# Node tiles of 124 rows instead of 128 in a four-layer graph kernel, without products of one row, and with the adjacency's row sums moved

## The reference

```python
# layer 0: two GRU cells, one on adj0 @ h, one on three attention heads (adj0 = adj without its diagonal)
edge_support = sum over heads of softmax(where(adj0 > 0, e_plus, -inf)) * adj0 @ hW, divided by 3
# layer 1: degree-normalised product
adj_norm = rowsum**-0.5 * adj * rowsum**-0.5 ; out = (adj_norm @ x) @ W.T + b
# layer 2: two attention heads over (adj + I) > 0, softmax over a row, elu
# layer 3: four attention heads over adj > 0.5, softmax over a column, bias
```

## Time and profile before

| | |
|---|---|
| median of 3 runs | 2648.63 us (2644.78 to 2657.8) |
| profiled execution, its own time | 2668.64 us |
| its span, first to last instruction | 2666.8 us |
| busy: PE / DVE / ACT / POOL | 2231.1 / 1563.6 / 768.5 / 252.2 us |
| mean granted TensorE clock | 0.882 of full speed |
| moved by DMA | 271.72 MB, mean 102 GB/s |

### The profile page before, as it was taken

One profiled execution on the slowest core, in us unless ns is written; L12 is line 12 of the kernel. 1 busy time (PEld: TensorE's weight loads), 2 busy tenths in 40 slices (PEclk: granted clock), 3 DMA queues, 4 the chain that ended last, 5 costly groups with the idle time before them and its releaser, 6 DMA issues. The chain is left out here.

```text
span 2666.8 us, 25438 instructions
## 1 busy us (share of the span) xinstructions
PE 2231.1 (84%) x9760; PEld 1184.0 (44%) x9760; DVE 1563.6 (59%) x2517; ACT 768.5 (29%) x1013; POOL 252.2 (9%) x128
## 2 busy tenths in 40 slices
PE   4889997068989999996999679977999845999991
PEld 2445555023434343445655334446999431222231
DVE  3323331566666766642577743345777256989787
ACT  0122221487777787743222100001000010000000
POOL 0000000000000000000000000000000005656440
PEclk9989995579999999998999889988989567989895
DMA  3366552334444444336000044421000004323211
GB/s 121 146 200 208 198 188 89 127 139 149 158 145 157 153 157 160 115 115 205 1 0 1 0 111 132 131 68 43 9 17 9 30 22 156 95 73 94 58 53 42
DMA packets 131908, 271.72 MB, mean 102 GB/s; under 512 B 14044, under 2 KB 44506, under 8 KB 127922
## 3 DMA queue, kind: packets, MB, share of 16 engines
q1 hardware_dynamic: 113458, 240.71, 28.4%
q10 hardware_dynamic: 18324, 29.34, 2.9%
HBM read 226.64 MB, written 43.37 MB: 101 GB/s over the span
## 5 line engine op out<-in xcount | busy, mean ns | idle before, releaser
L706 PE MATMUL banks<-arena 128*128 128x512 f32 (+3 forms) x1584 | 650.7, 570 | 57.8 <-DVE arena L1262 55.5
L706 PEld LDWEIGHTS banks<-arena 128*128 128x128 f32 (+1 forms) x1584 | 294.1, 199 | 412.7 <-issue 401.8
L1480 DVE SCALAR_TENSOR_TENSOR arena<-arena 128x1024 f32<-128x1024 f32 (+3 forms) x264 | 323.6, 1300 | 38.8 <-PE banks L842 20.2
L1262 DVE TENSOR_TENSOR arena<-arena 128x1536 f32<-128x1536 f32 (+2 forms) x132 | 206.8, 1567 | 170.6 <-ACT arena L964 170.5
L803 PE MATMUL banks<-arena 128*128 128x129 f32 (+2 forms) x1936 | 266.5, 300 | 5.1 <-DVE arena L1437 5.1
L803 PEld LDWEIGHTS banks<-arena 128*128 128x128 f32 (+2 forms) x1936 | 237.7, 202 | 36.8 <-issue 26.8
L765 PE MATMUL banks<-arena 128*128 128x512 f32 (+2 forms) x528 | 209.5, 548 | 45.6 <-DVE arena L1355 44.1
L667 PE MATMUL banks<-arena 128*128 128x512 f32 (+2 forms) x528 | 244.3, 591 | 0.0
L830 PE MATMUL banks<-arena 128*64 128x512 f32 (+3 forms) x1056 | 228.1, 570 | 12.8 <-DVE arena L1480 12.8
L572 POOL TENSOR_SCALAR arena<-arena 128x1024 bf16<-128x1024 f32 (+1 forms) x66 | 210.4, 3189 | 144.6 <-DVE arena L1480 136.8
L1437 DVE SCALAR_TENSOR_TENSOR arena<-arena 128x512 f32<-128x512 f32 (+2 forms) x264 | 169.9, 686 | 89.6 <-PE banks L803 77.0
(11 more groups left out here) (177 smaller groups left out, 1959.4 us busy)
## 6 DMA issues: line engine op xcount, KB each, us to landing
arena<-adj_T SPq DMA_DIRECT2D x210, 256.0 KB, 3.1
arena<-hw_rows SPq DMA_DIRECT2D x126, 384.0 KB
arena<-in_adj SPq DMA_DIRECT2D x21, 1354.0 KB
adj_T<-arena ACTq DMA_DIRECT2D x105, 256.0 KB, 2.6
arena<-in_adj SPq DMA_DIRECT2D x25, 1024.0 KB
arena<-in_adj SPq DMA_DIRECT2D x42, 512.0 KB
hw_rows<-arena SPq DMA_DIRECT2D x1, 8064.0 KB
arena<-in_adj SPq DMA_DIRECT2D x21, 330.0 KB
```

What stands on the lines that cost most here:

```text
L706: ins = PE.matmul(bank(2 * (c % 2) + f)[:, 0:wid(c)], hs[0:kp(t), n % 3, h * D + f * P:h * D + (f + 1) * P], E[0:kp(t), n % 3, h, 0:wid(c) ...
L1262: V.tensor_tensor(e, e, strips[n % 4][0:k, 0:w].unsqueeze(1).to_broadcast([k, H0, w]), ALU.mult).then_inc(s["p_ok"], 1)
L1480: V.scalar_tensor_tensor(PM3[0:k, n % 2, h, 0:w], r3_bc[0:k, h, c * WW:c * WW + w], smalls[0:k, 4, h * T + t:h * T + t + 1], mask3[0:k, n ...
```

## The change

A new constant R = 124 takes the place of P wherever P meant the rows of a node tile. T stays 22, but the last tile has 104 rows instead of 20; a chunk has W = 496 columns instead of 512, and the last one 228 instead of 148. The numbers of units, of products and of transfers stay as they are. Stage 3 keeps its chunks of 1024 columns. `opened` now multiplies 128 rows of zeros and closes itself (`start=True, stop=True`), `closed` is gone, and stage 2 has no opening product at all: the first product into a bank carries `start`. `row_sum` on ACT is gone; instead VectorE reduces each block of stage A to four partial sums, and the reader of the next block waits for it (`summed`).

```diff
+R = 124
-T = -(-N // P)
-TAIL = N - (T - 1) * P
+T = -(-N // R)
+TAIL = N - (T - 1) * R
 RPC = 4
-W = RPC * P
+W = RPC * R
...
-WW = 2 * W
+BANK = 512
+WW = 2 * BANK
...
 def kp(t):
-    return P if t < T - 1 else TAIL
+    return R if t < T - 1 else TAIL
...
         def load_nodes(eng, dst, src, s):
-            load(eng, dst[:, 0:T - 1, :], src[0:(T - 1) * P, :].rearrange("(t p) d -> p t d", p=P), s)
-            load(eng, dst[0:TAIL, T - 1, :], src[(T - 1) * P:N, :], s)
+            load(eng, dst[0:R, 0:T - 1, :], src[0:(T - 1) * R, :].rearrange("(t p) d -> p t d", p=R), s)
+            load(eng, dst[0:TAIL, T - 1, :], src[(T - 1) * R:N, :], s)
...
             if i >= 2:
                 sp.wait_ge(sw["A"]["transposed"], WideLoad(i - 2).units_after)
+                sp.wait_ge(sw["A"]["summed"], i - 1)
...
-            load(sp, arow[0:kp(i), :], adj[i * P:i * P + kp(i), :], b_in)
+            load(sp, arow[0:kp(i), :], adj[i * R:i * R + kp(i), :], b_in)
...
         def opened(b):
-            PE.matmul(bank(b), zrow[0:1, 0:P], zrow[0:1, :], start=True, stop=False)
-
-        def closed(b):
-
-            return PE.matmul(bank(b), zrow[0:1, 0:P], zrow[0:1, :], start=False, stop=True)
+            PE.matmul(bank(b), zrow[:, 0:P], zrow, start=True, stop=True)
...
                         ins = PE.matmul(bank(b0 + k // 3)[0:nr, (k % 3) * (C2 + 1):(k % 3 + 1) * (C2 + 1)],
-                                        PM2[0:kp(t), n % 3, h, r * P:r * P + nr], proj2[0:kp(t), t, h, :],
-                                        start=False, stop=False, skip_group_check=True)
-                if t == T - 1:
-                    for b in range(3):
-                        ins = closed(b0 + b)
+                                        PM2[0:kp(t), n % 3, h, r * R:r * R + nr], proj2[0:kp(t), t, h, :],
+                                        start=k // 3 not in begun, stop=t == T - 1, skip_group_check=True)
+                        begun.add(k // 3)
...
-            def row_sum(i):
-                act.wait_ge(b_diag, i + 1)
-                S.activation(arow[0:kp(i), :], arow[0:kp(i), :], ACT.Copy, accum_out=rowsum[0:kp(i), i:i + 1]
-                             ).then_inc(b_sum, 1)
...
+            def row_sums(ld):
+                dve.wait_ge(s["wide_in"][ld.buf], ld.landed)
+                if ld.k == ld.c:
+                    dve.wait_ge(s["diag_ok"], ld.c * RPC + tiles_in(ld.c))
+                if ld.c < CH - 1:
+                    ins = V.tensor_reduce(rpart[0:R, ld.c * RPC:(ld.c + 1) * RPC, ld.k], ablk[0:R, ld.buf, :, 0:ld.width], AX_X, ALU.add)
+                else:
+                    for r, nr in enumerate(rows_in(ld.c)):
+                        ins = V.tensor_reduce(rpart[0:nr, ld.c * RPC + r, ld.k:ld.k + 1], ablk[0:nr, ld.buf, r, 0:ld.width], AX_X, ALU.add)
+                ins.then_inc(s["summed"], 1)
...
+                if t % 4 == 3 or t == T - 1:
+                    row_sums(WideLoad(c * LOADS * 2 + t // 4))
...
                 if h == 0:
-                    dve.wait_ge(b_sum, i + 1)
+                    dve.wait_ge(b_diag, i + 1)
```

More of the change, by code:

```diff
@@ L189, in build @@
         E21 = sb(T, 3, 2 * H0 + 1)
+        rpart = sb(T, LOADS * 2)
         ur = sb(T, 2 * H0)
@@ L290, in build @@
         l3_mask, l3_g, l3_scaled, l3_p, l3_mm, l3_read = (sem(f"l3_{s}") for s in ("mask", "g", "scaled", "p", "mm", "read"))
-        b_in, b_diag, b_sum, b_rowfree, b_negm, b_exp = (sem(f"b_{s}") for s in ("in", "diag", "sum", "rowfree", "negm", "exp"))
+        b_in, b_diag, b_rowfree, b_negm, b_exp = (sem(f"b_{s}") for s in ("in", "diag", "rowfree", "negm", "exp"))
         den_log, nst_ok, nst_ps, nst_sb, m_out = (sem(s) for s in ("den_log", "nst_ok", "nst_ps", "nst_sb", "m_out"))
@@ L368, in unit_loads @@
                 sp.wait_ge(s["p_ok"], n - 3)
-            load(sp, strips[n % 4][0:kp(t), 0:wid(c)], adj_T[t * P:t * P + kp(t), c * W:c * W + wid(c)], s["blk_in"][n % 4])
+            load(sp, strips[n % 4][0:kp(t), 0:wid(c)], adj_T[t * R:t * R + kp(t), c * W:c * W + wid(c)], s["blk_in"][n % 4])
             if n >= 3:
                 sp.wait_ge(s["mm_done"], n - 2)
-            load(sp, hs[0:kp(t), n % 3, :], hw_rows[t * P:t * P + kp(t), :], hs_in[n % 3])
+            load(sp, hs[0:kp(t), n % 3, :], hw_rows[t * R:t * R + kp(t), :], hs_in[n % 3])
         def maxima_row(sp, c):
@@ L377, in maxima_row @@
             sp.wait_ge(nst_sb, c + 1)
-            load(sp, m_rows[c:c + 1, 0:H0 * nt * P].rearrange("a (k p) -> (a k) p", p=P), rows_s[0:H0 * nt, :], m_out)
+            load(sp, m_rows[c:c + 1, 0:H0 * nt * R].rearrange("a (k p) -> (a k) p", p=R), rows_s[0:H0 * nt, 0:R], m_out)
             sp.wait_ge(m_out, 16 * (c + 1))
@@ L382, in maxima_row @@
                 sp.wait_ge(sw["C"]["clamp_ok"], T * (c - 1))
-            load(sp, m_bc[:, c % 2, :, 0:wid(c)], m_rows[c:c + 1, 0:H0 * nt * P].rearrange(
+            load(sp, m_bc[:, c % 2, :, 0:wid(c)], m_rows[c:c + 1, 0:H0 * nt * R].rearrange(
                 "a (h n) -> (a h) n", h=H0)[:, 0:wid(c)].partition_broadcast(P), mbc_in)
@@ L391, in strip1 @@
                 sp.wait_ge(l1_mask, n - 3)
-            load(sp, strips1[0:kp(t), n % 4, 0:wid(c)], adj_T[t * P:t * P + kp(t), c * W:c * W + wid(c)], l1_in[n % 4])
+            load(sp, strips1[0:kp(t), n % 4, 0:wid(c)], adj_T[t * R:t * R + kp(t), c * W:c * W + wid(c)], l1_in[n % 4])
         def strip3(sp, n):
@@ L398, in strip3 @@
                 sp.wait_ge(l3_mask, n - 2)
-            load(sp, strips3[0:kp(t), n % 3, 0:wide(c)], adj[t * P:t * P + kp(t), c * WW:c * WW + wide(c)], l3_in[n % 3])
+            load(sp, strips3[0:kp(t), n % 3, 0:wide(c)], adj[t * R:t * R + kp(t), c * WW:c * WW + wide(c)], l3_in[n % 3])
         def sp_rows(sp, k, dram, heads, bc):
             sp.wait_ge(rows[k][2], 1)
-            load(sp, dram.rearrange("h (t p) -> (h t) p", p=P), (d_s if k == "d" else rows_s)[0:heads * T, :], rows[k][3])
+            load(sp, dram.rearrange("h (t p) -> (h t) p", p=R), (d_s if k == "d" else rows_s)[0:heads * T, 0:R], rows[k][3])
             sp.wait_ge(rows[k][3], 16)
@@ L671, in products_A @@
                         pe.wait_ge(s["e21_free"], c - 1)
-                    PE.matmul(bank(be), zrow[0:1, 0:P], zrow[0:1, :], start=True, stop=False)
+                    opened(be)
                 pe.wait_ge(s["mask_ok"], n + 1)
@@ L819, in _ @@
                 c, t = divmod(n, T)
-                halves = [(v, min(W, wide(c) - v * W)) for v in range(-(-wide(c) // W))]
+                halves = [(v, min(BANK, wide(c) - v * BANK)) for v in range(-(-wide(c) // BANK))]
                 for h in range(0, H3, 2):
@@ L1170, in _ @@
             dve.wait_ge(s["e21_free"], CH)
+            dve.wait_ge(s["summed"], CH * LOADS * 2)
+            for nr, ts in FULL:
+                V.tensor_reduce(rowsum[0:nr, ts], rpart[0:nr, ts], AX_X, ALU.add)
             for nr, ts in FULL:
```

95 lines of the change are left out of this document (41 added, 54 removed).

## The result

The change makes the kernel slower: 3527.19 us median (3519.86 to 3533.47) against 2652.18 for the kernel before (four executions), a ratio of 1.33 with the 95% interval [1.3254, 1.3346]. The forecast was 3440 us, range 3370 to 3760. The profiled execution has a span of 3518.1 us, 851 more than before, where the sum said 791. Between the medians the difference is 875, as the profiled execution before was 16 us slower than its median and the one after 7 us faster.

The account below looks back on a forecast made before the run. The prediction took TensorE, with VectorE in stage 3, to bound the kernel before, and four DMA engines to bound stages A, C and 1 after. Terms 330 + 359 + 65 + 75 - 30 - 8 = +791 gave 3440 us, range 3370 to 3760.

Parts of the forecast that it names:

- How many engines: Node-row transfers: engines are the largest divisor of the rows up to 16, so 124 rows use the same four.
- What one engine moves: Long strips: 24.3 GB/s for one never-idle engine, 97.2 for four; bad end 82.9.
- the 22 us that I had added for waits: Stage A: added to 653 us of transfers for start and drained end, giving 675 us for 345, +330.
- Stage C: Attention of layer 0: transfers, broadcasts and 45 us of SP waits make 1157 us for 798, +359.
- Stage 1: 29.5 MB on four engines take 295 us, plus 13 for start and end: 308 for 243.5, +65.
- Exposed transfers: x, heads and result, 1 KB packets, uncovered: 33.6 us each at 80.4 GB/s for 8.9, together +75.
- One-row products: Stages 2 and 3: fewer products and less half clock save 30 us (ends 0 and 50) and 8 us.
- five boundaries cost 3.4 each: Stage 2: the clock at 0.5 for 6.8 us at a chunk boundary costs 3.4 us at each of five.
- Row sums: Moving them to VectorE in stage A and off ACT in stage C costs nothing under the slower transfers.
- Sixteen engines: Rival: 124-row transfers still spread widely, stages stay bound by TensorE, 89 us gained, 2560 us; chance 0.05.
- The half clock: Rival: TensorE, waiting for transfers, falls to half clock; stages C and 1 together +304, 3745 us; chance 0.09.
- The slower engines: Rival: each engine gives only 20.7 GB/s, four 82.9; stages A, C and 1 longer, +1142, 3790 us; chance 0.12.

Follow-up runs that it names:

- The dose run: Kernel before, stage 1 strip loads split by chunk to use 16, 7, 5, 4 or 3 engines; chunks 0 to 4 took 41, 42, 45, 58 and 75 us.
- e10_tiles: Changed kernel, with x, the heads and the result moved one tile a transfer instead of one transfer each; 3467.04 us.
- e4_products: Kernel before with only the one-row products changed as in the change, tiles of 128 rows kept; 2599.34 us, ratio 0.9801.
- e9_spread: As e5_overlap, but stage A's row sums made one row tile at a time behind each unit's masks; 2536.77 us, ratio 0.9545.
- e5_overlap: Changed kernel, with loads of 128 rows at a stride of 124 and only stores cut in two (112 + 12); 2554.64 us, ratio 0.9627.
- e8_both: Kernel before, tiles of 128 rows, with both the row sums moved and the one-row products changed; 2590.58 us, ratio 0.9781.

## Why the prediction was right, point by point

The mechanism was the one forecast, and it is shown. The size is good in part by luck: stages A, C, 1 and the exposed transfers came out 103 us above their terms, the one-row products gained 40 us more than theirs, and the rest is 3, which leaves 60 in the profiled executions.

*How many engines.* Right, and shown in four ways: the share that stops at 0.25 to 0.27, the packet counts of stage 1, the return to about the speed of before with 112 + 12 rows, and the old tiling made slow with 124 + 4. The inference from three odd row counts (88, 6, 20) to 124 carried the whole forecast. The Trainium skill ("DMA: Bandwidth & Descriptors", "Why a DMA increments its semaphore by 16 and not by 1") has the rule, with the largest divisor up to 16 and always the lowest-numbered engines. The dose run agrees with the divisor at 7, 5, 4 and 3 engines. Stage A's 0.26 over two queues agrees with both taking the same ones; that they are the lowest-numbered no run shows.

*What one engine moves.* Nearly right. I took 97.2 GB/s for four, which with the faster last tile makes 100 for the whole. Stage C's loop had just that, stage 1 had 94 with its start and end and 101 in its middle. Stage A had 92 over its 708 us, 33 above the forecast, and its share was 0.24 or more in every part: the 22 us that I had added for waits were not waits, and the rate was what I had too high. It was 95 in the middle 580 us. In its first 74 us, where the projection goes out with the 21-block shape, it was 81 GB/s:

```profile
145.60:220.00 74.40, 26.69 (x116) 15.22 (x117) 10.21 (x18) 4.58 (x8) 1.67 (x4) 0.64 0.25 81
```

*Stage C.* +391 for +359. The first four rows took 129 us where they took 95; I had said that the faster row without the sum and the slower load cancel. That is the step that failed there, by 34 us. The first exponential comes 15 us later after the start of the stage than before: the small store of `e_rows` and its way back, issued behind the first row, take 18 us for 6. In the rest of the window the strips of the first three units are queued ahead of the second row, the engines stand at 0.25, and even the fourth row comes 21 us behind the third, where I had 16 to 17.

*Stage 1.* +71 for +65.

*Exposed transfers.* +107 for +75 (38, 36 and 33 each for 25): the rate was 61 to 66 GB/s and not 80.4. I had put it down to packets of 1 KB; e10_tiles shows 92 with the same packets in another shape.

*One-row products.* The mechanism was right in the main, the size too small: -57 and -21 us measured in stages 2 and 3 for -30 and -8. The step that failed is "five boundaries cost 3.4 each": four cost that or less, but behind the fifth the clock stayed at half through the whole last chunk, 55 us, which is some 27 us by itself (half of it, an estimate from the two rows of e4_products). I gave part of the fall to the 20-row tile; in stage 2 e4_products shows no fall with that tile in place, and 42 and 20 us from the products alone. The other 15 us of stage 2 are the new tiling's, mostly in its last chunk. In stage 3 I counted only the products' own time and forgot what the clock does after them, though it is said of stage 2 in the same paragraph.

*Row sums.* Costed at nothing, and under the transfers this cannot be told apart. On 16 engines both halves of it were wrong: the sums cost stage A 23 us (I said some 10 at most), and leaving them off ACT gives stage C 43 (I said 15). In stage A I had looked for late masks; the waits that the traces show are for blocks that load late (e9_spread). In stage C the 15 us for the first four rows were right, 16 measured; the loop, which I had put at nothing, gave 26. ACT's slack of 492 busy in 639 us misled me. My reading is that ACT and VectorE hand the rows to each other in turn, so that a 2.6 us instruction between them is on the path although neither is full; what is shown is that TensorE waits 13 us less for VectorE and is busy 12 us less at its higher clock.

*Rivals.* Sixteen engines did not happen. What it named as the gain that would be left, 89 us, was 100 in e5_overlap, from partly other terms. The half clock happened in part: 0.74 in stage A and 0.83 in C, but TensorE's work stayed under the transfers' time, and in stage 1 the clock was 0.97. The slower engines happened by a small part, 92 for 97.

## What to carry to other kernels

Before a tile's row count is changed, look at its largest divisor up to 16: 128, 112 and 96 give 16 DMA engines, 124 gives 4, and a prime above 16 gives 1 by the same rule (that last one was not run). Where a tile must have an awkward height, load a round number of rows and leave the rest unused, and cut only the stores, as e5_overlap does. Read the DMA share with that in mind: a share of 0.45 is well hidden on 16 engines and is nearly twice too much for 4, and a flat 0.25 can be four engines that never rest.

## What the runs showed that I had not expected

- Behind products of a single row TensorE's granted clock fell while TensorE stayed busy, at 21 of 25 chunk boundaries of stage 2 and at none without them: a mean of 0.83 in the sweep of stage 2 with them, 0.97 without, and 59 us in the whole kernel (e4_products).
- A last chunk of 148 columns, with tiles of 20 rows, stands at half clock through stage A and takes 54 us; one of 228 columns and 104 rows has 0.98 and takes 33 (e8_both, e5_overlap).
- Cutting each node transfer into two parts cost 135 us (5.2%) with all engines in use, 63 us of it in the stage where SP issues two loads a unit.
- Loads of one shape (124 partitions, 21 blocks of 1 KB) ran at 15 GB/s an engine on four engines; over 128 partitions and 16 engines the same shape ran at 19.5. Taking them tile by tile gave 23 on four engines and 41 us back.
- A reduction of 2.2 us behind every fourth unit cost 14 us more than four of a quarter the length, the work being the same (e9_spread against e5_overlap). TensorE never waited for VectorE there; it waited for the next block, whose load the reduction released.
